# D times xc added by DVE, the gate multiplied by POOL: a diagonal matmul taken out of a state-space kernel

## Chip, cores and metric

The kernel runs on one core of one Trainium2 chip. The metric is the device time of one execution in microseconds. The engines are called as in the profile: PE is TensorE (its matmuls; PEld its weight loads), DVE is VectorE, ACT is ScalarE, POOL is GpSimd, SP is SyncE, which issues the DMAs.

## What is computed

16 samples of 64 x 64 positions and 96 channels pass two layers with residuals. Layer 0 normalizes by groups, resamples, and applies a quadratic between two matrices. Layer 1 is a selective state-space layer over the L = 4096 positions of a sample, with 192 inner channels and 16 states:

```python
xs, z = split(u @ W_in.T)
xc = silu(conv3(xs) + conv_b)
dt, Bm, Cm = split(xc @ W_x.T)
delta = softplus(dt @ W_dt.T + b_dt)
h = exp(delta * A) * h + delta * Bm * xc        # for each position in turn
y = sum_n(h * Cm) + xc * D
y = y * silu(z)
out = x + y @ W_out.T
```

The change concerns the last three lines: `+ xc * D`, the product with `silu(z)`, and when the product with `W_out` comes.

## The kernel before

**Tiling.** A sample is 8 chunks of T = 512 positions, so there are 128 chunks in all. A chunk has NU = 24 units: 192 channels x 16 states are 24 tiles of 128 rows by 512 positions. Three units form a group, 12 units a half (96 channels, `hf` 0 and 1).

**One unit.** ACT makes `av` (the exponential, L883). At the first unit of a group PE spreads B over 128 rows into the one PSUM bank `pb` (`spread_b`, L746), and DVE multiplies it with `rep_u` into `b3` for all three units (L1022, called b in the trace). For each unit DVE runs the scan into `hs` (L1028), POOL multiplies it by C into `hc` (L1069), and after each group PE sums over the states into the PSUM bank `py` (`reduce`, L757). At the start of each half PE first puts `diag(D)` times `xcs` into `py` (L754). When a half's four groups are summed, DVE multiplies `py` by `zs` = silu(z) into `xcs` (`gate`, L1036): half 0 after the scan of unit 15, half 1 after the scan of unit 3 of the next chunk.

**Order of work.** Every engine has one queue, and each is written out by one walk over chunks and units (`run`): the unit's own work, `c_part` (the chunk before), `a_part` (the chunk two ahead), and then the steps of a plan whose row is due. A row is a chunk's number times 24 plus a unit. `LAG` puts the steps later on the other engines than on PE (ACT by 6 units, DVE 3, POOL 2, SP 1). PE takes `spread_b` at units 1, 4, 7 and so on for the group that comes next, `reduce` at units 5 (group 0), 8, 11 and so on; groups 6 and 7 fall to units 23 and 2. `spread_b` must wait until DVE has read `pb` (`dve_bu`), and `b3` must wait for `pb`.

**Steps of the plan.** They share a ring of three PSUM banks `cb`; step i waits until step i - 3's bank is free. The steps are the resampling and the two matrices of layer 0 for samples ahead (S, W and D steps; W_f is L671, W_2 is L676, W_up is L665), the next chunks' X (L710), Z (L716), DBC (L720) and DT (L725) matmuls, with X and Z together at rows 8 and 9 of each chunk (the batch), and OUT, the output projection of the chunk before (L737 and L738), at row 6. OUT waits for both gates of its chunk (`dve_y`). ACT copies its bank to `os_` (L802), and SP stores it at its unit 13. The last sample has no S, W or D steps beside it, the one before it no S steps and W steps only until row 86.

The line numbers and functions:

Of the kernel before, what the change touches and what calls it, by code (L numbers as in the profile page):

```python
# [9 lines left out]
ALU = mybir.AluOpType  # L10
ACT = mybir.ActivationFunctionType

NS, HH, WW, C = 16, 64, 64, 96
# [9 lines left out]
NC8 = L // T  # L23
NJ, NQ = DI // 32, DSTATE // 4
NU = NJ * NQ
# [3 lines left out]
LEAD = 2  # L29
# [5 lines left out]
AT = {  # L35
    "pe": dict(pb=1, red=5),
    "act": dict(xn=8, mid=23, batch=BATCH + 6),
    "dve": dict(y0=15, y1=3),
    "pool": dict(u=23, bc=(16, 21)),
    "sp": dict(rd=(1, 2, 3, 5), ru=(6, 8, 10, 12), cs=(15, 16, 17, 18), dl=20, du=4, x1=21, out=13),  # L40
}
# [65 lines left out]
def plan_of(kind):  # L107
    rows = stage_rows(kind in ("first", "full"), kind in ("first", "full"), kind in ("first", "full", "tail"),
                      kind in ("first", "full", "tail"))
    for k in range(NC8):  # L110
        if kind != "last" or k < NC8 - LEAD:
            rows += mamba_rows(k)
        elif k == NC8 - LEAD:
            rows += mamba_rows(k, True)
        rows.append((k * NU + 6, ("PAD", -1) if kind == "first" and k == 0 else ("OUT", k)))
    if kind == "last":
        rows.append((NC8 * NU + 6, ("OUT", NC8)))
    return padded(rows)
# [22 lines left out]
def build(nc, A):  # L141
    ctx = ExitStack()
    with ctx:  # L143
        def sb(name, shape, dt=F32):
            return ctx.enter_context(nc.sbuf_tensor(name, shape, dt))
# [4 lines left out]
        def sem(name):  # L150
            return ctx.enter_context(nc.semaphore(name))
# [33 lines left out]
        dskip = sb("dskip", [C, 2])  # L185
        ddiag = sb("ddiag", [C, 2, C])
        selb = sb("selb", [C, NQ, 128], BF16)
# [102 lines left out]
        pe_red = sem("pe_red")  # L290
        dve_y = sem("dve_y")
        out_st = sem("out_st")

# [31 lines left out]
        SETUP_STEPS = 3  # L325
        N_SETUP = 14
        BEFORE = [alone([("SLD", 0)] + s_steps() + [("SG1", 0), ("SG2", 0)]),
# [76 lines left out]
        def count(sm, v):  # L404

            return max(v, 0)
# [194 lines left out]
        def _(pe):  # L601
# [125 lines left out]
            def out(st, k, bank):  # L727

                G = st.s * NC8 + k
                p = (k - 1) % 4  # L730
                pe.wait_ge(dve_y, count(dve_y, G * 2))
                pe.wait_ge(x1o_ld, count(x1o_ld, G * 16))
                for b in range(4):
                    tb = slice(128 * b, 128 * b + 128)
                    o = bank[:, C * b:C * b + C]
                    for t in range(2):
                        pe.matmul(o, xcs[:, p, t, tb], wo[:, t, :], start=(t == 0), stop=False)  # L737
                    mm = pe.matmul(o, x1o[:, tb], ident[0:C, 0:C], start=False, stop=True)  # L738
                return mm
# [8 lines left out]
            def reduce(s, k, g):  # L748
                G = s * NC8 + k
                hf, q = g // NQ, g % NQ  # L750
                pe.wait_ge(pool_hc, count(pool_hc, G * NU + 3 * g + 3))
                if q == 0:
                    pe.wait_ge(dve_y, count(dve_y, G * 2 + hf))
                    pe.matmul(py[0:C, :], ddiag[:, hf, :], xcs[:, k % 4, hf, :], start=True, stop=False,  # L754
                              skip_group_check=True)
                for j in range(3):
                    mm = pe.matmul(py[32 * j:32 * j + 32, :], rsel[:, :], hc[:, (3 * g + j) % NHC, :],  # L757
                                   start=False, stop=(q == NQ - 1), skip_group_check=True)
                mm.then_inc(pe_red, 1)
# [22 lines left out]
        def _(act):  # L782
# [63 lines left out]
            def batched(st, key, i):  # L846
# [11 lines left out]
                elif name == "Z":  # L858
                    t = key[2]
                    act.wait_ge(dve_y, count(dve_y, (G2 - LEAD) * 2))  # L860
                    act.wait_ge(pe_conv, st.done(i))
# [55 lines left out]
        def _(dve):  # L917
# [8 lines left out]
            def setup(ins):  # L926
                n_set[0] += 1
                ins.then_inc(setup_v, 1)
                dve.wait_ge(setup_v, count(setup_v, n_set[0]))
# [8 lines left out]
            for tap in range(3):  # L938
                setup(dve.tensor_tensor(wtap[:, tap, :, :], winx.rearrange("c (t p) -> c t p", t=2),
                                        cwb.rearrange("c (p t k) -> c k t p", t=2, k=3)[:, tap], ALU.mult))  # L940
            for t in range(2):
                setup(dve.tensor_scalar(ddiag[:, t, :], ident[0:C, 0:C], dskip[:, t:t + 1], None, ALU.mult))
            dve.wait_ge(setup_a, count(setup_a, 2))
# [69 lines left out]
            def unit(s, k, n):  # L1013
# [16 lines left out]
                if n == AT["dve"]["y0"]:  # L1030
                    gate(G, k, 0)

            def gate(G, k, hf):

                dve.wait_ge(pe_red, count(pe_red, G * NG + (hf + 1) * NQ))
                dve.tensor_tensor(xcs[:, k % 4, hf, :], zs[:, k % 2, hf, :], py[0:C, :], ALU.mult).then_inc(dve_y, 1)  # L1036

            def c_part(st, k, n):
                G = st.s * NC8 + k
                if n == AT["dve"]["y1"] and not (G < 1):  # L1040
                    gate(G - 1, (k - 1) % NC8, 1)

# [3 lines left out]
        def _(pool):  # L1046
# [56 lines left out]

            run(lambda row: row[0] + LAG["pool"], unit, step, a_part, lambda st, k, n: None)

# [67 lines left out]
```

## Time and profile before

| | |
|---|---|
| median of 3 runs | 7185.96 us (7182.05 to 7199.08) |
| the profiled execution | 7219.16 us, span 7217.5 us |
| busy, share of the span | PE 89%, DVE 82%, ACT 66%, POOL 63% |
| mean granted TensorE clock | 0.912 |
| first `b3` of the first chunk | 331.8 us |

The time is that of a whole execution; the span runs from the first to the last instruction in the profile. A busy share is the sum of an engine's instructions without overlaps. [...] The idle time in front of a group of instructions, with the engine that ended it, tells who waited for whom.

### The profile page before, as it was taken

The numbers are of one execution on the slowest core, as the hardware profiler recorded it, in microseconds if no ns is written. First come the engines' busy times: TensorE is split into PE (matmuls) and PEld (weight loads), VectorE is DVE, ScalarE is ACT, GpSimd is POOL, SyncE is SP. The second block draws the span as 40 slices with busy tenths as digits, with TensorE's granted clock in tenths as the row PEclk, the third lists the DMA queues.
The fourth block names the chain that finished last, engine by engine and source line by source line (L and its number), as shares of the span: only waits on it lengthen the run. The fifth ranks groups of instructions, "written<-read, shape, count | busy, mean of one in ns | idle before, by whom it ended". The sixth has DMA issues, their size and how long they took to land. (4 is left out here: it accounts for less than half of the span.)

```text
span 7217.5 us, 97516 instructions
## 1 busy us (share of the span) xinstructions
PE 6447.3 (89%) x32099; PEld 3299.1 (46%) x32099; DVE 5943.6 (82%) x4956; ACT 4794.1 (66%) x7986; POOL 4577.4 (63%) x4516
## 2 busy tenths in 40 slices
PE   7898998999898998999999899998999989898765
PEld 5545444444444444444444444444444444444211
DVE  0188888888888888888888888888888888889898
ACT  4576767667676776766667666676766767667554
POOL 0166666666666766667666666666766666677676
PEclk8998989999898998999999898998989999899776
DMA  3465655655655555565655555666555655555552
GB/s 89 112 151 134 146 141 129 148 136 146 148 136 141 140 143 137 145 147 131 150 130 147 143 134 140 138 150 144 136 146 132 150 137 145 144 129 142 121 122 68
DMA packets 805815, 983.15 MB, mean 136 GB/s; under 512 B 391258, under 2 KB 417542, under 8 KB 805318
## 3 DMA queue, kind: packets, MB, share of 16 engines
q1 hardware_dynamic: 805318, 976.92, 56.4%
q8 instruction: 264, 4.33, 0.3%
q14 instruction: 233, 1.91, 0.1%
HBM read 717.71 MB, written 259.00 MB: 135 GB/s over the span
## 5 line engine op out<-in xcount | busy, mean ns | idle before, releaser
L1069 POOL TENSOR_TENSOR hc<-hs,cs 128x512 f32<-128x512 f32 x3072 | 3843.5, 1269 | 2272.8 <-DVE hs L1028 1880.1
L1028 DVE TENSOR_TENSOR_SCAN hs<-av,state,b 128x512 f32<-128x512 f32 x2688 | 3282.4, 1264 | 83.5 <-DVE b L1022 2.7
L1022 DVE TENSOR_TENSOR b<-rep_u,pb 128x1536 f32<-128x1536 f32 x1024 | 1802.8, 1761 | 785.3 <-PE pb L746 721.2
L883 ACT ACTIVATE av<-rep_d,nega 128x512 f32<-128x512 f32 x3072 | 2129.2, 713 | 139.4 <-DVE hs L1028 134.9
L757 PE MATMUL py<-hc,rsel 128*32 128x512 f32 x6144 | 1227.4, 678 | 27.3 <-POOL hc L1069 27.2
L676 PEld LDWEIGHTS cb<-w2c,g 128*98 128x98 f32 x9600 | 937.6, 178 | 330.2 <-issue 267.9
L671 PE MATMUL cb<-xu,w1a 96*128 96x392 f32 x2400 | 1039.9, 529 | 50.1 <-ACT dlt L873 31.0
L676 PE MATMUL cb<-w2c,g 128*98 128x96 f32 x9600 | 990.2, 264 | 83.2 <-issue 55.4
L833 ACT ACTIVATE g<-cb,b1a 128x392 f32<-128x392 f32 x1200 | 695.7, 580 | 205.3 <-PE cb L671 189.5
L746 PE MATMUL pb<-bc,selb 96*128 96x512 bf16 x1024 | 416.4, 407 | 370.0 <-DVE b L1022 368.6
L710 PE MATMUL cb<-xn,wtap 96*96 96x512 f32 x1536 | 701.0, 606 | 0.3 <-DVE spare L966 0.3
L671 PEld LDWEIGHTS cb<-xu,w1a 96*128 96x128 f32 x2400 | 409.4, 194 | 547.8 <-issue 350.6
L1028 DVE TENSOR_TENSOR_SCAN hs<-av,zero_state,b 128x512 f32<-128x512 f32 x384 | 468.1, 1264 | 12.2 <-ACT av L883 0.6
L710 PEld LDWEIGHTS cb<-xn,wtap 96*96 96x96 f32 x1536 | 243.5, 165 | 468.7 <-issue 467.3
L857 ACT ACTIVATE xcs<-cb,tapb 96x512 f32<-96x512 f32 x256 | 174.9, 683 | 409.9 <-PE cb L710 409.9
L757 PEld LDWEIGHTS py<-hc,rsel 128*32 128x32 f32 x6144 | 161.8, 113 | 620.0 <-issue 449.4
L665 PE MATMUL cb<-up_h,t1r 128*96 128x196 f32 x1600 | 362.6, 351 | 50.7 <-DVE b1a L1000 46.8
L826 ACT ACTIVATE vr<-cb 98x384 f32<-98x384 f32 x400 | 194.3, 486 | 305.4 <-PE cb L676 304.0
L746 PEld LDWEIGHTS pb<-bc,selb 96*128 96x128 bf16 x1024 | 107.1, 105 | 618.2 <-DVE b L1022 393.3
L754 PE MATMUL py<-xcs,ddiag 96*96 96x512 f32 x512 | 296.3, 663 | 95.2 <-DVE xcs L1036 71.9
L737 PE MATMUL cb<-wo,xcs 96*128 96x96 f32 x2048 | 346.5, 297 | 0.8 <-issue 0.8
L826 ACT ACTIVATE xu<-cb 96x392 f32<-96x392 f32 x400 | 194.1, 485 | 221.5 <-PE cb L665 219.5
(102 smaller groups left out, 6525.5 us busy)
## 6 DMA issues: line engine op xcount, KB each, us to landing
rep_d<-delta_scratch SPq DMA_DIRECT2D x512, 384.0 KB, 6.2
rep_u<-deltax_scratch SPq DMA_DIRECT2D x512, 384.0 KB, 6.1
cs<-c_scratch SPq DMA_DIRECT2D x512, 256.0 KB, 6.1
delta_scratch<-dlt SPq DMA_DIRECT2D x128, 384.0 KB, 3.1
deltax_scratch<-dlt SPq DMA_DIRECT2D x128, 384.0 KB, 8.1
t_scratch<-t1s SPq DMA_DIRECT2D x128, 300.0 KB
t1r<-t_scratch SPq DMA_DIRECT2D x160, 240.0 KB, 5.0
rr<-v_scratch SPq DMA_DIRECT2D x256, 150.0 KB
```

Of the source, the lines that this page charges most:

```text
L665: mm = pe.matmul(bank[0:C, e * 2 * GH:(e + 1) * 2 * GH], t1r[:, m % 2, i2 % 5, :], up_h[:, :], start=True, stop=True)
L671: mm = pe.matmul(bank[:, 0:BC], w1a[:, 128 * f:128 * f + 128], xu[:, b % 2, :], start=True, stop=True)
L676: mm = pe.matmul(bank[0:GH, C * j:C * j + C], g2[:, b % 2, f, GH * j:GH * j + GH], w2c[:, f, :], start=(f == 0), stop=(f == NF - 1))
L710: mm = pe.matmul(bank[0:C, :], wtap[:, tap, t, :], xn[:, k2 % 2, tap:tap + T], start=(tap == 0), stop=(tap == 2))
L746: pe.matmul(pb[:, :], selb[:, g % NQ, :], bc3[:, k % 4, :], start=True, stop=True).then_inc(pe_b, 1)
L757: mm = pe.matmul(py[32 * j:32 * j + 32, :], rsel[:, :], hc[:, (3 * g + j) % NHC, :], start=False, stop=(q == NQ - 1), skip_group_check=True)
L826: act.activation(out, src, ACT.Copy).then_inc(fr, 1)
L833: act.activation(g2[:, b % 2, f, :], bank[:, 0:BC], ACT.Square, bias=b1a[:, f:f + 1]).then_inc(fr, 1)
L883: act.activation(av[:, n % NAV, :], rep_d[:, k % 2, j, :], ACT.Exp, scale=nega[:, q, j:j + 1])\
L1022: dve.tensor_tensor(b3[:, :, :], rep_u[:, k % 2, 3 * hf:3 * hf + 3, :], pb[:, None, :].broadcast_to([128, 3, T]), ALU.mult).then_inc(dve_b ...
L1028: dve.tensor_tensor_scan(hs[:, n % NHS, :], av[:, n % NAV, :], b3[:, n % 3, :], start, ALU.mult, ALU.add)\
L1069: pool.tensor_tensor(hc[:, n % NHC, :], hs[:, n % NHS, :], cs[:, k % 2, g % NQ, :], ALU.mult)\
```

## The change

`ddiag` and its two setup operations go, and with them the matmul L754; the first `reduce` of a half now starts the accumulation. DVE's `gate` becomes `skip`: it reads `py`, adds `D * xcs` in the same instruction and writes `xcs`. POOL multiplies both halves of `xcs` by `zs` in one instruction of 96 x 1024, at its unit 4 of the next chunk, behind that unit's product. OUT and ACT's Z wait for POOL's new semaphore `pool_y` in place of `dve_y`. OUT goes from row 6 to row 7 and SP's store from unit 13 to 14; PE's queue at row 7 has `spread_b` of group 3 first and then the steps, so OUT is now behind it.

```diff
-    "pool": dict(u=23, bc=(16, 21)),
-    "sp": dict(rd=(1, 2, 3, 5), ru=(6, 8, 10, 12), cs=(15, 16, 17, 18), dl=20, du=4, x1=21, out=13),
+    "pool": dict(u=23, bc=(16, 21), gate=4),
+    "sp": dict(rd=(1, 2, 3, 5), ru=(6, 8, 10, 12), cs=(15, 16, 17, 18), dl=20, du=4, x1=21, out=14),
...
-        rows.append((k * NU + 6, ("PAD", -1) if kind == "first" and k == 0 else ("OUT", k)))
+        rows.append((k * NU + 7, ("PAD", -1) if kind == "first" and k == 0 else ("OUT", k)))
...
-                pe.wait_ge(dve_y, count(dve_y, G * 2))
+                pe.wait_ge(pool_y, count(pool_y, G))
                 pe.wait_ge(x1o_ld, count(x1o_ld, G * 16))
...
                 if q == 0:
                     pe.wait_ge(dve_y, count(dve_y, G * 2 + hf))
-                    pe.matmul(py[0:C, :], ddiag[:, hf, :], xcs[:, k % 4, hf, :], start=True, stop=False,
-                              skip_group_check=True)
                 for j in range(3):
                     mm = pe.matmul(py[32 * j:32 * j + 32, :], rsel[:, :], hc[:, (3 * g + j) % NHC, :],
-                                   start=False, stop=(q == NQ - 1), skip_group_check=True)
+                                   start=(q == 0), stop=(q == NQ - 1), skip_group_check=True)
...
                     t = key[2]
-                    act.wait_ge(dve_y, count(dve_y, (G2 - LEAD) * 2))
+                    act.wait_ge(pool_y, count(pool_y, G2 - LEAD))
...
-            def gate(G, k, hf):
+            def skip(G, k, hf):
 
                 dve.wait_ge(pe_red, count(pe_red, G * NG + (hf + 1) * NQ))
-                dve.tensor_tensor(xcs[:, k % 4, hf, :], zs[:, k % 2, hf, :], py[0:C, :], ALU.mult).then_inc(dve_y, 1)
+                dve.scalar_tensor_tensor(out=xcs[:, k % 4, hf, :], in0=xcs[:, k % 4, hf, :], scalar=dskip[:, hf:hf + 1],
+                                         in1=py[0:C, :], op0=ALU.mult, op1=ALU.add).then_inc(dve_y, 1)
...
+            def c_part(st, k, n):
+                G = st.s * NC8 + k
+                if n == AT["pool"]["gate"] and G >= 1:
+
+                    pool.wait_ge(dve_y, count(dve_y, G * 2))
+                    pool.tensor_tensor(xcs[:, (k - 1) % 4], xcs[:, (k - 1) % 4], zs[:, (k - 1) % 2], ALU.mult).then_inc(pool_y, 1)
```

## Rows read from the trace of the kernel before

**Rows 1.** The page, part 1: busy us of the whole execution, share, instructions.

```profile
PE 6447.3 (89%) x32099; PEld 3299.1 (46%) x32099; DVE 5943.6 (82%) x4956; ACT 4794.1 (66%) x7986; POOL 4577.4 (63%) x4516
```

**Rows 2.** The waits: who waited for whom, us in total, times, longest.

```profile
DVE b L1022 <- PE pb L746: 721.2, 321, 8.2
...
PE pb L746 <- DVE b L1022: 368.6, 169, 5.4
```

**Rows 3.** Groups of instructions by shape: busy and mean ns, idle before, releasers.

```profile
L1028 DVE TENSOR_TENSOR_SCAN hs<-av,state,b 128x512 f32<-128x512 f32 x2688 | 3282.4, 1264 | 83.5 <-DVE b L1022 2.7 <-POOL state L1073 0.4
...
L1102 POOL TENSOR_TENSOR dlt<-dlt,xcs 96x1024 f32<-96x1024 f32 x128 | 301.5, 2355 | 26.4 <-DMA delta_scratch<-dlt 24.3 <-PE py L757 2.1
L754 PE MATMUL py<-xcs,ddiag 96*96 96x512 f32 x512 | 296.3, 663 | 95.2 <-DVE xcs L1036 71.9 <-POOL hc L1069 21.7
...
L1036 DVE TENSOR_TENSOR xcs<-zs,py 96x512 f32<-96x512 f32 x256 | 169.4, 662 | 31.0 <-PE py L757 31.0
...
L984 DVE SCALAR_TENSOR_TENSOR vv<-dm,mv 96x1 f32<-96x1 f32 x32 | 34.4, 1074 | 1.1
```

**Rows 4.** Windows: full samples, then from 6680 us: busy by engine, clock, DMA, GB/s.

```profile
763.50:6680.00 5916.50, 5417.95 (x27270) 2793.33 (x27273) 5064.20 (x4191) 4059.74 (x6790) 3909.88 (x3852) 0.93 0.59 141
6680.00:7217.50 537.50, 353.18 (x1198) 111.53 (x1192) 480.73 (x377) 276.93 (x405) 375.36 (x374) 0.72 0.44 102
```

**Rows 5.** Timeline of the last sample, chunk at 6919 us: start us, us, engine, instruction.

```profile
6928.91 1.99 PE L754 MATMUL py<-xcs,ddiag 96*96 96x512 f32 x2 [1.42 <-DVE xcs L1036]
...
6930.04 2.49 POOL L1069 TENSOR_TENSOR hc<-hs,cs 128x512 f32<-128x512 f32 x2 [0.36 <-DVE hs L1028]
...
6930.83 1.93 PE L757 MATMUL py<-hc,rsel 128*32 128x512 f32 x6
6931.23 1.76 DVE L1022 TENSOR_TENSOR b<-rep_u,pb 128x1536 f32<-128x1536 f32 x1
...
6932.69 0.89 PE L737 MATMUL cb<-wo,xcs 96*128 96x96 f32 x4
...
6935.65 0.38 PE L746 MATMUL pb<-bc,selb 96*128 96x512 bf16 x1
...
6936.95 5.39 PE L710 MATMUL cb<-xn,wtap 96*96 96x512 f32 x12
...
6944.31 1.76 DVE L1022 TENSOR_TENSOR b<-rep_u,pb 128x1536 f32<-128x1536 f32 x1 [2.02 <-PE pb L746]
```

**Rows 6.** Windows in the same chunk, before and after the clock rises.

```profile
6919.60:6933.10 13.50, 7.33 (x18) 1.40 (x19) 13.02 (x11) 4.80 (x8) 12.62 (x13) 0.50 0.82 185
6933.20:6944.30 11.10, 11.10 (x51) 5.34 (x52) 8.90 (x7) 5.10 (x8) 7.71 (x8) 1.00 0.87 183
```

**Rows 7.** PE in a chunk with the output projection at 1.2 GHz: timeline, window.

```profile
5791.05 1.06 PE L737 MATMUL cb<-wo,xcs 96*128 96x96 f32 x4
...
5796.17 0.63 PE L746 MATMUL pb<-bc,selb 96*128 96x512 bf16 x1
...
5789.90:5796.30 6.40, 6.40 (x34) 6.26 (x32) 0.00 (x0) 0.47 (x1) 0.21 (x2) 0.50 0.57 151
```

**Rows 8.** Timeline of a sample's last chunk, from 5504 us.

```profile
5514.41 1.10 PE L754 MATMUL py<-xcs,ddiag 96*96 96x512 f32 x2 [1.30 <-POOL hc L1069]
5514.45 3.72 POOL L1069 TENSOR_TENSOR hc<-hs,cs 128x512 f32<-128x512 f32 x3
...
5515.92 1.76 DVE L1022 TENSOR_TENSOR b<-rep_u,pb 128x1536 f32<-128x1536 f32 x1
...
5517.19 0.58 PE L737 MATMUL cb<-wo,xcs 96*128 96x96 f32 x4
```

**Rows 9.** Timeline around units 17 to 24 of the chunk at 5606 us.

```profile
5646.78 1.02 PE L754 MATMUL py<-xcs,ddiag 96*96 96x512 f32 x2
...
5651.77 1.76 DVE L1022 TENSOR_TENSOR b<-rep_u,pb 128x1536 f32<-128x1536 f32 x1 [1.18 <-PE pb L746]
...
5659.89 1.76 DVE L1022 TENSOR_TENSOR b<-rep_u,pb 128x1536 f32<-128x1536 f32 x1 [1.19 <-PE pb L746]
```

More of the change, by code:

```diff
@@ L114, in plan_of @@
             rows += mamba_rows(k, True)
-        rows.append((k * NU + 6, ("PAD", -1) if kind == "first" and k == 0 else ("OUT", k)))
+        rows.append((k * NU + 7, ("PAD", -1) if kind == "first" and k == 0 else ("OUT", k)))
     if kind == "last":
-        rows.append((NC8 * NU + 6, ("OUT", NC8)))
+        rows.append((NC8 * NU + 7, ("OUT", NC8)))
     return padded(rows)
@@ L185, in build @@
         dskip = sb("dskip", [C, 2])
-        ddiag = sb("ddiag", [C, 2, C])
         selb = sb("selb", [C, NQ, 128], BF16)
@@ L291, in build @@
         dve_y = sem("dve_y")
+        pool_y = sem("pool_y")
         out_st = sem("out_st")
@@ L325, in build @@
         SETUP_STEPS = 3
-        N_SETUP = 14
+        N_SETUP = 12
         BEFORE = [alone([("SLD", 0)] + s_steps() + [("SG1", 0), ("SG2", 0)]),
@@ L940, in _ @@
                                         cwb.rearrange("c (p t k) -> c k t p", t=2, k=3)[:, tap], ALU.mult))
-            for t in range(2):
-                setup(dve.tensor_scalar(ddiag[:, t, :], ident[0:C, 0:C], dskip[:, t:t + 1], None, ALU.mult))
             dve.wait_ge(setup_a, count(setup_a, 2))
@@ L1030, in unit @@
                 if n == AT["dve"]["y0"]:
-                    gate(G, k, 0)
-            def gate(G, k, hf):
+                    skip(G, k, 0)
+            def skip(G, k, hf):
                 dve.wait_ge(pe_red, count(pe_red, G * NG + (hf + 1) * NQ))
-                dve.tensor_tensor(xcs[:, k % 4, hf, :], zs[:, k % 2, hf, :], py[0:C, :], ALU.mult).then_inc(dve_y, 1)
+                dve.scalar_tensor_tensor(out=xcs[:, k % 4, hf, :], in0=xcs[:, k % 4, hf, :], scalar=dskip[:, hf:hf + 1],
+                                         in1=py[0:C, :], op0=ALU.mult, op1=ALU.add).then_inc(dve_y, 1)
             def c_part(st, k, n):
@@ L1040, in c_part @@
                 if n == AT["dve"]["y1"] and not (G < 1):
-                    gate(G - 1, (k - 1) % NC8, 1)
+                    skip(G - 1, (k - 1) % NC8, 1)
             run(lambda row: row[0] + LAG["dve"], unit, step, lambda st, k, n: None, c_part)
@@ L1102, in a_part @@
                     pool.tensor_tensor(dlt[:, :, :], dlt[:, :, :], xcs[:, k2 % 4], ALU.mult).then_inc(pool_u, 1)
-            run(lambda row: row[0] + LAG["pool"], unit, step, a_part, lambda st, k, n: None)
+            def c_part(st, k, n):
[3 more added lines that the diff above has]
+                    pool.tensor_tensor(xcs[:, (k - 1) % 4], xcs[:, (k - 1) % 4], zs[:, (k - 1) % 2], ALU.mult).then_inc(pool_y, 1)
+            run(lambda row: row[0] + LAG["pool"], unit, step, a_part, c_part)
 def resampling():
```

## Prediction

> **What bounds the kernel now.** I read four views in this order. The page's first part says that no engine is full: PE 89%, DVE 82%, POOL 63% [rows 1]. So the bound must change hands inside each chunk, and the waits say between whom: DVE waits 721 us for `pb` from PE (321 times), and PE waits 369 us for DVE to release the single `pb` buffer (169 times) [rows 2]. Who is late where, the timelines tell. A chunk (24 units, 8 groups, 128 chunks) has two halves. In groups 0 to 2 DVE leads and PE waits for it. Then PE has the output projection, reduction 1 and the batch of X and Z matmuls in a row, and group 4's `b` is late in every chunk: in the chunk at 6919 us DVE idles 2.02 us before it [rows 5]. So what PE does between the first gate of a chunk and group 4 is on the path; most of what it does in groups 0 to 2 is not. The last view is TensorE's clock: 0.93 on average while a sample has all its side work, 0.72 from 6680 us on [rows 4]. In the chunk at 6919 us it is 0.50 (1.2 GHz) up to 6933.1 us, where DVE waits for nobody, and 1.00 (2.4 GHz) right after, in the stretch that is on the path [rows 6]. Where the clock rises thus matters as much as how much work there is.
>
> **The change, part by part.**
>
> *The diagonal matmuls go.* 256 of them (512 records). The two records took 1.02 us at 2.4 GHz [rows 9] and 1.99 us at 1.2 GHz [rows 5]; the group's sum is 296 us [rows 3]. As PE's work overlaps by some 0.07 us from group to group, each is worth 0.95 us of PE's time at 2.4 GHz. The second one of a chunk (unit 17) lies where PE comes late to groups 7 and 0: the chunk at 5606 us shows DVE idle 1.18 us before group 7's `b` and 1.19 us before the next group 0's [rows 9]. The same two places in the eight chunks from 5553 to 5987 us: in four chunks such a wait is over 1 us in at least one of them, in two about 0.6 us, in two nothing; so 4 x 0.95 + 2 x 0.5 = 4.8 us a sample, and with 14 samples that have side work -67 us. Ends: 0, if the time goes into other waits, and 8 x 0.95 x 14 = -106 us. I take -67.
>
> *The first diagonal matmul and the moved output, at an unchanged clock.* The projection goes from row 6 (before `pb` of group 3) to row 7 (behind it). So PE no longer fills the time until `b` of group 2 has released `pb`. At 5504 us and later: `b` ends at 5515.92 + 1.76 = 5517.68. PE began the projection at 5517.19; without the diagonal it is there 1.0 us earlier, at 5516.2, and now stands until 5517.7, 1.5 us [rows 8]. Then come `pb` and a W step, and the projection waits for POOL: unit 4's product ends at 5514.45 + 2.5 = 5516.95, the new multiply has the shape of L1102, 2.36 us [rows 3], so 5519.3 us. It starts 2.1 us later than before and has `pb` and that W step (0.8 us together, an estimate) behind it already, so group 4 comes 1.3 us later. In the other seven chunks the waits come to 0 to 1.3 us and are paid with the diagonal's 0.95 us: from a gain of 0.9 (fourth chunk, where PE comes late anyway) to a loss of 0.2. Sum over a sample about +0.3 us with this chunk, x 14 = +4 us; ends -14 and +28 us.
>
> *The clock.* This is the term on which I decide. In the chunk at 6919 us PE works from 6928.91 us without a pause: diagonal 1.99 us, reduction 0 1.93 us, and the clock rises at about 6933.1 us, as the projection has begun; projection, reduction 1 and batch then run at 2.4 GHz [rows 5, 6]. After the change PE has reduction 0 alone, then stands 2.2 us until `b` of group 2 ends at 6932.99 us, does `pb`, and starts the projection at 6930.04 + 1.26 + 2.36 = 6933.7 us, 1.0 us later than before. Does the projection itself raise the clock? Rows say no: from 5789.9 to 5796.3 us PE was busy without a gap, nearly all of it projection, and the clock stayed 0.50; the projection took 5796.17 - 5791.05 = 5.1 us in place of 6935.65 - 6932.69 = 3.0 us [rows 5, 7]. So I expect +1.0 (later start), +2.1 (projection at 1.2 GHz), +0.9 (reduction 1, 1.93 us in place of 1.06) and about +1 for the part of the batch before the rise (between 0 and the batch's whole 5.4 us): 5.0 us for each of some 9 chunks without W and S work at the end. +45 us; ends +9 (clock as before) and +90.
> [...]
> In the 14 full samples the same can happen wherever PE now pauses before the projection. Most exposed is each sample's last chunk, [rows 8]: pauses of 1.30 us before reduction 0, then 1.5 us and a short third one, with little work between. Next are the seventh and the second with 0.9 to 1.6 us. If the clock falls there, the loss is that of above without its first term, 4 to 5 us. I take 1.3 such losses a sample at 4.5 us: 6 us x 14 = +84 us; ends 0 and 3 a sample, +189 us.
>
> *DVE's new operation.* `skip` reads one tile of SBUF and one of PSUM, as the gate did (662 ns) and as the scan does [rows 3]; it has two arithmetic steps and a pointer scalar more. A scan has a pointer scalar too and takes its 1264 ns next to a busy POOL. I take 0 to 60 ns for each of 256, half of them where DVE is on the path: +8 us; ends 0 and +15.
> The nearest operation of the same name, L984, takes 1074 ns for one element [rows 3]. [...]
>
> *POOL.* 128 multiplies of 2.36 us more, 302 us; POOL goes from 63% to 67%. They stand before unit 5's product and put it off by 2.4 us. Reduction 1 needs it, but now follows the projection, 2.8 us or more later; group 3's scans need its buffers some 2 us after it is ready. Cost nothing; without that cover it would be up to 2.4 us a chunk. ACT's Z (unit 14) waits for POOL's product of unit 4, done long before. The queues that OUT is moved past: ACT has one exponential more before it, SP stores `os_` one unit later; both ran ahead. At the very end the multiply stands alone on the path: +2 us.
>
> **Sum.** -67 + 4 + 45 + 84 + 8 + 2 = +76 us. The profiled execution took 7219.2 us (span 7217.5), so its like would take about 7295; the median of the three runs is 33 us lower, and I add the difference to it: 7186 + 76 = 7262 us.
>
> **Rivals.**
> *Less work for PE, faster.* All as above but for the clock, which keeps its level in full samples: -67 + 4 + 9 to 24 + 8 + 2 = -44 to -29 us, and with the second diagonal paying in every chunk -85: 7100 to 7157, say 7140 us. For it: PE is the busiest engine and DVE waits for it twice as long as the other way [rows 1, 2]. Against: the pauses of [rows 8]. It decides when a sample has fewer than about 0.6 such losses (0.6 x 4.5 x 14 = 38 us).
> *They cancel.* Between half a loss and one a sample, or DVE as the bound everywhere: 7165 to 7207 us, say 7186.
> [...]
> *The change does not do what it says:* the diagonal goes, but the rows saved are waited away at `pb`. That is the case "cancel" without clock, included there.
>
> **Chances.** Slower by the clock 0.55, the port 0.02, cancel 0.16, faster 0.27. 0.3% (22 us) is about what a measurement here can tell from no change. Likeliest 7262, its own range 7210 to 7350. Faster cases reach down to 7100; I leave 1 in 10 out below 7120 and 1 in 10 above 7350.
>
> **What the next profile would show.** Right: no L754; in the chunks after 6680 us the clock is still 0.50 while the projection runs, it takes about 5 us there, and the idle time before group 4's `b` grows from 2.0 to about 7 us; the idle time before group 3's vanishes; DVE's total wait for `pb` rises from 721 us towards 800, PE's wait for DVE too; the mean clock falls below 0.91. POOL's multiply 2.36 us, `skip` 660 to 720 ns. The wait before groups 7 and 0 shrinks by about 1 us where it was larger. Wrong, if the clock rises before the projection after all, or if the last chunk of a sample keeps 2.4 GHz: then 7140. [...]

## The result, and the profile after

| | median | runs |
|---|---|---|
| before | 7186.33 us | 5 |
| after | 7463.32 us | 5 (7429.8 to 7471.32) |

The ratio is 1.0366, 95% interval 1.0347 to 1.0386: 277 us slower. The direction is as forecast, the size is 3.6 times the forecast's 76 us. The profiled execution of after took 7429.8 us (span 7428.0), 210.6 us more than the one of before; it is the quickest of its five, so the traces hold 211 of the 277 us. The mean granted clock, TensorE's share of its full speed, fell from 0.912 to 0.873. Where the prediction and the expectations write 1.2 and 2.4 GHz, the windows show a granted clock of 0.50 and of 1.00 [rows 6]; no view gives a frequency. One of before's later executions took 7324 us at a clock of 0.868; it is set apart as slow and stands in no ratio below.

The page of after, part 1, and the waits that answer to [rows 2]:

```profile
PE 6458.6 (87%) x31587; PEld 3386.2 (46%) x31587; DVE 5957.0 (80%) x4954; ACT 4798.8 (65%) x7986; POOL 4866.4 (66%) x4644
```

```profile
DVE b L1018 <- PE pb L746: 903.6, 271, 15.6
...
PE pb L746 <- DVE b L1018: 481.4, 277, 5.4
```

PE has 512 matmuls fewer and is busy 11 us longer: the diagonal's 296 us [rows 3] are gone, and the remaining matmuls take 308 us more. They are the same instructions at a mean granted clock of 0.873 in place of 0.912: L737, for one, is busy 413.5 us where it was 346.5. DVE waits 182 us more for `pb` in fewer waits (271, before 321); the longest is 15.6 us where it was 8.2. Added up by the group of the `b` that waits, the idle time of DVE before group 4's grew from 415 to 719 us, the one before group 3's fell from 134 to 44, and the one before groups 7 and 0 together from 141 to 102. So the loss lies where the projection and the batch are. The groups of after, by shape:

```profile
L737 PE MATMUL cb<-wo,xcs 96*128 96x96 f32 x2048 | 413.5, 339 | 12.2 <-issue 11.7
...
L1106 POOL TENSOR_TENSOR xcs<-xcs,zs 96x1024 f32<-96x1024 f32 x128 | 301.3, 2354 | 2.7 <-DVE xcs L1032 2.7
...
L694 PE MATMUL cb<-xt,wtot 96*96 96x256 f32 x512 | 194.5, 468 | 55.8 <-DMA rr<-v_scratch 51.2 <-DMA xt<-xt_scratch 2.8
L1032 DVE SCALAR_TENSOR_TENSOR xcs<-xcs,dskip,py 96x512 f32<-96x512 f32 x256 | 184.9, 722 | 31.8 <-PE py L755 31.8
```

and L694 in before:

```profile
L694 PE MATMUL cb<-xt,wtot 96*96 96x256 f32 x512 | 187.8, 454 | 15.9 <-DMA rr<-v_scratch 10.7 <-DMA xt<-xt_scratch 3.3
```

The multiply takes the 2.36 us of the forecast, `skip` 722 ns (60 more than the gate, the upper end). The surprise is L694, the first matmul of a D step: over the whole run it waits 51.2 us for its DMA `rr`, before 10.7 us. The windows answer to [rows 4]; the clock is the number after POOL's busy time:

```profile
763.50:6860.00 6096.50, 5437.72 (x26925) 2873.35 (x26924) 5093.19 (x4206) 4071.66 (x6802) 4169.09 (x3974) 0.89 0.58 137
6860.00:7428.00 568.00, 356.80 (x1098) 120.28 (x1096) 470.32 (x367) 273.97 (x398) 393.53 (x378) 0.62 0.40 93
```

The clock of 0.93 has become 0.89 in the full samples, and 0.72 has become 0.62 at the end.

**Where the time went.** The traces were cut into chunks, from the start of group 0's `b` to the next. Places in a sample are counted from 1 (first chunk, sixth chunk), samples and chunks of the run from 0. "Projection" is the time from OUT's first matmul to its last: in after's trace 2.8 to 2.9 us in the 67 chunks where the granted clock was 1.00 over all of it, 5.3 to 5.4 in the 44 where it was 0.50 (16 had both). Means over the 13 samples 1 to 13, by place in the sample, us:

| chunk of the sample | 1 | 2 | 3 | 4 | 5 | 6 | 7 | 8 | sum |
|---|---|---|---|---|---|---|---|---|---|
| before, chunk | 54.2 | 53.7 | 51.6 | 56.3 | 63.7 | 54.5 | 50.0 | 51.0 | 435.1 |
| after, chunk | 52.2 | 52.5 | 51.1 | 56.1 | 64.8 | 62.5 | 52.9 | 54.2 | 446.3 |
| before, OUT starts at | 14.1 | 14.0 | 14.1 | 16.0 | 23.6 | 15.1 | 15.6 | 13.9 | |
| after, OUT starts at | 16.0 | 14.9 | 14.5 | 17.7 | 24.5 | 21.2 | 16.7 | 15.1 | |
| before, projection | 2.8 | 2.8 | 2.8 | 2.8 | 5.1 | 2.8 | 2.8 | 3.4 | |
| after, projection | 2.8 | 2.8 | 2.8 | 2.8 | 5.3 | 5.3 | 3.8 | 4.9 | |

13 x 11.2 = 146 us. The last sample but one takes 427.8 us in place of 404.2, the first seven chunks of the last 365.5 in place of 332.5: 57 us. Together 202 of 211 us; 8 lie in sample 0 and at the ends. The largest entry is the sixth chunk, 8.0 us in each of these samples. This is one of them (it starts at 5950.18 us) on PE in after's timeline:

```profile
5965.00 0.39 PE L746 MATMUL pb<-bc,selb 96*128 96x512 bf16 x1 [0.44 <-DVE b L1018]
5965.23 0.82 PE L671 MATMUL cb<-xu,w1a 96*128 96x392 f32 x2
5969.37 1.14 PE L694 MATMUL cb<-xt,wtot 96*96 96x256 f32 x2 [3.32 <-DMA rr<-v_scratch]
5970.31 1.49 PE L698 MATMUL cb<-dn_w,rr 100*96 100x96 f32 x8
5971.59 1.06 PE L737 MATMUL cb<-wo,xcs 96*128 96x96 f32 x4
...
5976.85 1.93 PE L755 MATMUL py<-hc,rsel 128*32 128x512 f32 x6
5978.70 7.32 PE L710 MATMUL cb<-xn,wtap 96*96 96x512 f32 x12
5985.86 1.88 PE L716 MATMUL cb<-xn,winz 96*96 96x512 f32 x4
```

and on DVE:

```profile
5987.99 1.76 DVE L1018 TENSOR_TENSOR b<-rep_u,pb 128x1536 f32<-128x1536 f32 x1 [13.38 <-PE pb L746]
```

The same chunk in before's timeline (it starts at 5831.52 us), PE and then DVE:

```profile
5846.60 0.58 PE L737 MATMUL cb<-wo,xcs 96*128 96x96 f32 x4
...
5849.25 0.38 PE L746 MATMUL pb<-bc,selb 96*128 96x512 bf16 x1
5849.47 0.82 PE L671 MATMUL cb<-xu,w1a 96*128 96x392 f32 x2
5851.69 0.64 PE L694 MATMUL cb<-xt,wtot 96*96 96x256 f32 x2 [1.40 <-DMA rr<-v_scratch]
...
5853.93 5.39 PE L710 MATMUL cb<-xn,wtap 96*96 96x512 f32 x12
```

```profile
5861.29 1.76 DVE L1022 TENSOR_TENSOR b<-rep_u,pb 128x1536 f32<-128x1536 f32 x1 [5.40 <-PE pb L746]
```

The reader is to see the order. Row 7 holds `pb`, then a W step (L671), then a D step (L694, L698) that waits for `rr`. Before, the projection stood ahead of all of it and filled most of the time until `rr` came; the D step waited 1.40 us. After, the projection is queued behind the wait, now 3.32 us, starts 6 us later, and comes out of the pause at a granted clock of 0.50. Windows of after, over the pause with what PE did just ahead of it, over the projection, and (last two) in the end-of-run chunk shown next:

```profile
5965.10:5968.90 3.80, 0.95 (x3) 0.32 (x2) 3.80 (x4) 1.57 (x3) 3.69 (x4) 1.00 0.95 199
5970.50:5977.20 6.70, 6.70 (x36) 6.37 (x37) 4.02 (x4) 0.66 (x2) 0.00 (x0) 0.50 0.74 169
...
7114.60:7132.70 18.10, 15.74 (x44) 7.82 (x45) 13.08 (x10) 4.43 (x7) 13.38 (x13) 0.50 0.71 160
7132.90:7137.00 4.10, 4.10 (x11) 1.34 (x9) 0.00 (x0) 1.31 (x3) 0.00 (x0) 1.00 0.13 27
```

That chunk (start 7105.20 us) answers to [rows 5]; timeline of after:

```profile
7114.70 1.93 PE L755 MATMUL py<-hc,rsel 128*32 128x512 f32 x6 [1.49 <-DVE xcs L1032]
...
7117.04 2.35 POOL L1106 TENSOR_TENSOR xcs<-xcs,zs 96x1024 f32<-96x1024 f32 x1
...
7118.83 0.61 PE L746 MATMUL pb<-bc,selb 96*128 96x512 bf16 x1 [2.21 <-DVE b L1018]
...
7119.50 1.14 PE L737 MATMUL cb<-wo,xcs 96*128 96x96 f32 x4
...
7124.83 1.93 PE L755 MATMUL py<-hc,rsel 128*32 128x512 f32 x6
...
7126.69 8.46 PE L710 MATMUL cb<-xn,wtap 96*96 96x512 f32 x12
...
7137.12 1.76 DVE L1018 TENSOR_TENSOR b<-rep_u,pb 128x1536 f32<-128x1536 f32 x1 [9.05 <-PE pb L746]
```

PE stands 1.49 and 2.21 us, the projection starts as POOL's multiply ends, and the granted clock stays at 0.50 until 7132.8 us, through the projection, reduction 1 and the first 6.1 of L710's 8.46 us. Group 4's `b` waits 9.05 us for `pb` where it waited 2.02 [rows 5].

### The profile page after: what moved, and what is told of

Same layout as the page of the kernel before. It is cut to its first block and busy times, and to the rows that moved or that the text cites. A ratio compares the mean times of both kernels' runs of the same rounds, so it can differ in the third digit from the quotient of the medians.

```text
span 7428.0 us, 96643 instructions
## 1 busy us (share of the span) xinstructions
PE 6458.6 (87%) x31587; PEld 3386.2 (46%) x31587; DVE 5957.0 (80%) x4954; ACT 4798.8 (65%) x7986; POOL 4866.4 (66%) x4644
## 3 DMA queue, kind: packets, MB, share of 16 engines
q1 hardware_dynamic: 805318, 976.92, 55.2%
## 5 line engine op out<-in xcount | busy, mean ns | idle before, releaser
L755 PE MATMUL py<-hc,rsel 128*32 128x512 f32 x6144 | 1278.4, 704 | 120.0 <-DVE xcs L1032 72.3
L676 PEld LDWEIGHTS cb<-w2c,g 128*98 128x98 f32 x9600 | 960.7, 182 | 359.3 <-issue 241.1
L676 PE MATMUL cb<-w2c,g 128*98 128x96 f32 x9600 | 1014.7, 267 | 110.9 <-issue 54.9
L671 PE MATMUL cb<-xu,w1a 96*128 96x392 f32 x2400 | 1041.0, 530 | 49.2 <-ACT dlt L871 31.0
L710 PE MATMUL cb<-xn,wtap 96*96 96x512 f32 x1536 | 746.5, 638 | 0.0
L671 PEld LDWEIGHTS cb<-xu,w1a 96*128 96x128 f32 x2400 | 411.2, 195 | 548.2 <-issue 352.9
L710 PEld LDWEIGHTS cb<-xn,wtap 96*96 96x96 f32 x1536 | 259.2, 177 | 532.3 <-issue 532.0
L737 PE MATMUL cb<-wo,xcs 96*128 96x96 f32 x2048 | 413.5, 339 | 12.2 <-issue 11.7
L737 PEld LDWEIGHTS cb<-wo,xcs 96*128 96x128 f32 x2048 | 373.5, 253 | 46.0 <-issue 38.7
L800 ACT ACTIVATE os_<-cb 128x384 f32<-128x384 f32 x128 | 62.8, 490 | 482.8 <-PE cb L738 482.8
```

Of the source, the lines that this page charges most:

```text
L671: mm = pe.matmul(bank[:, 0:BC], w1a[:, 128 * f:128 * f + 128], xu[:, b % 2, :], start=True, stop=True)
L676: mm = pe.matmul(bank[0:GH, C * j:C * j + C], g2[:, b % 2, f, GH * j:GH * j + GH], w2c[:, f, :], start=(f == 0), stop=(f == NF - 1))
L710: mm = pe.matmul(bank[0:C, :], wtap[:, tap, t, :], xn[:, k2 % 2, tap:tap + T], start=(tap == 0), stop=(tap == 2))
```

## The experiments

Three theories were set against each other. *Clock:* the loss is TensorE running at a granted clock of 0.50 behind pauses that the change puts ahead of the projection. *Queue:* the projection stands behind something that waits. *POOL:* the projection or the Z copies wait for the new multiply. Row 6.5 stands for a place in row 7 behind `pb` of group 3 but ahead of that row's S, W and D steps. Each kernel was timed beside before, whose median in these rounds was 7192 to 7205 us, not 7186; the ratios and their intervals are the measure, and a difference of less than 20 us between two rows of the table says little. "Under 4 us" counts the projections, of the 104 in samples 1 to 13, that were.

| kernel | diagonal | OUT | multiply | median us | ratio, 95% | under 4 us |
|---|---|---|---|---|---|---|
| before | yes | row 6 | DVE | 7186 | | 89 |
| E13 | yes | 6.5 | DVE | 7243.56 | 1.0050 (1.0025, 1.0075) | 95 |
| E2 | yes | row 7 | DVE | 7322.39 | 1.0190 (1.0159, 1.0221) | 80 |
| E6 | no | row 6 | DVE | 7095.57 | 0.9861 (0.9828, 0.9895) | 97 |
| E8 | no | row 7 | DVE | 7428.34 | 1.0318 (1.0286, 1.0350) | 66 |
| E4 | yes | row 7 | POOL | 7397.37 | 1.0289 (1.0250, 1.0327) | 76 |
| E10 | yes | row 6 | POOL | 7401.82 | 1.0274 (1.0251, 1.0296) | 83 |
| after | no | row 7 | POOL | 7463 | 1.0366 (1.0347, 1.0386) | 59 |
| E1 | no | row 6 | POOL | 7432.00 | 1.0341 (1.0318, 1.0364) | 69 |
| E5 | no | 6.5 | POOL | 7393.32 | 1.0264 (1.0237, 1.0291) | 73 |
| E3 | no | row 6 | POOL, unit 3 | 7169.36 | 0.9951 (0.9931, 0.9970) | 88 |
| E9 | no | row 6 | POOL, by halves | 7110.63 | 0.9874 (0.9846, 0.9902) | 90 |
| E11 | no | row 6 | POOL, idle matmuls | 7296.07 | 1.0123 (1.0085, 1.0162) | 94 |
| E12 | no | row 6 | as E9, some idle matmuls | 7096.16 | 0.9847 (0.9819, 0.9874) | 95 |

**E1: after, the projection back in row 6.**

```diff
-    "pool": ..., "sp": dict(..., out=14),
+    "pool": ..., "sp": dict(..., out=13),
-        rows.append((k * NU + 7, ... ("OUT", k)))
+        rows.append((k * NU + 6, ... ("OUT", k)))
```

> The changed kernel with the output projection back in row 6 (and SP's store at unit 13); DVE's skip, POOL's multiply and the missing diagonal stay. Theory A, the place: with the changed kernel the projection lies behind that row's D step, which waits 3.3 us for a DMA in the sixth chunk of each sample, PE stands, and the clock is at 1.2 GHz when the projection starts (21.2 to 26.4 us of the chunk, b of group 4 at 36.6 in place of 28.9 us). With row 6 the sixth chunk gets about 8 us back and the fifth 1 us, 14 times: 7463 - 126 = about 7340 us, between 7300 and 7380. Not all comes back, since the projection still waits for POOL. Theory B, POOL: the projection waits for POOL's multiply wherever it stands, and in row 6 it holds up the spread of group 3 too: no gain, 7460 us or more. Theory C, less work for PE by itself lets the clock fall: no gain from the place, 7440 to 7480 us.

Measured: 7432.0, only 31 us under after and in none of the three ranges that were expected (7300 to 7380, 7460 or more, 7440 to 7480). The sixth chunk is back at 55.2 us, so the queue in it is gone; but the second takes 56.5 (before 53.7), the seventh 53.9, the eighth 56.3, with projections of 4.2, 4.1 and 5.3 us. What the projection now waits for is POOL, and PE stands meanwhile: the idle time before L737 without a named releaser is 162 us on PE's matmuls and 234 on their weight loads, in the kernel without the multiply (E6, below) 1 and 24. One place of E1's trace in the last sample ties it to POOL, whose multiply ends at 7111.64 + 2.34 = 7113.98 us:

```profile
7111.64 2.34 POOL L1106 TENSOR_TENSOR xcs<-xcs,zs 96x1024 f32<-96x1024 f32 x1
```

```profile
7114.08 1.14 PE L737 MATMUL cb<-wo,xcs 96*128 96x96 f32 x4 [2.87 <-issue]
```

**E2: before, the projection in row 7** (the reverse of E1's edit, on the old kernel).

> The kernel before with one edit: the output projection in row 7 (and SP's store at unit 14); diagonal matmuls and DVE's gate stay. Theory A, the place: the sixth chunk of each sample loses about 8 us as in the changed kernel, 14 x 8 = 112 us: about 7300 us, between 7260 and 7340; at the end of the run, where there is no side work, nothing, as diagonal and reduction 0 still raise the clock before the projection. Theory B, POOL, and theory C, less work for PE: neither is in this kernel, so 7186 us within 22 us.

Measured: +136 us with nothing else changed. Its sixth chunk takes 62.4 us (projection starts at 20.7, takes 5.3); the end-of-run chunks stay at 47.8 us, with the granted clock at 1.00 over their projections. In this execution the place alone costs the sixth chunk and little else; E13 shows an execution in which the end of the run pays too.

**E4: after, with the diagonal matmuls back on PE** (`skip` stays, with a scalar of zero; `ddiag` and its setup, not shown, come back too).

```diff
+                    pe.matmul(py[0:C, :], ddiag[:, hf, :], xcs[:, k % 4, hf, :], start=True, stop=False, ...)
-                                   start=(q == 0), stop=(q == NQ - 1), skip_group_check=True)
+                                   start=False, stop=(q == NQ - 1), skip_group_check=True)
-                dve.scalar_tensor_tensor(..., scalar=dskip[:, hf:hf + 1],
+                dve.scalar_tensor_tensor(..., scalar=zero2[:, hf:hf + 1],
```

> The changed kernel with the two diagonal matmuls of a chunk back on PE; DVE's skip stays the same instruction but its scalar is zero, so the output is the reference's and only PE's work differs. Clock theory (C, and part of A): in the chunks at the end of the run diagonal and reduction 0 keep PE at work together and the clock is up sooner; these chunks lose about 1 us in place of 5, some 9 x 4 = 36 us less, and the last chunks of samples some more; against it the second diagonal costs up to 2 us a chunk x 4 a sample again. Faster than the changed kernel, 7380 to 7440 us, with the chunks at the end near 49 us in place of 52 to 55. Rival, PE's work is what counts: each diagonal costs its 0.95 us where PE is late, 7463 + 60 to 120 us = 7520 to 7580 us.

Measured: 7397.4. More work for PE, 66 us less time than after. The gain is where projections are quick again (seventh chunk 51.3 us with a projection of 2.8, after 52.9 with 3.8; eighth 51.8 with 3.4, after 54.2 with 4.9); the chunks of the last sample did not change (51.9 to 54.9 us up to the sixth, in after 51.9 to 55.3), where 49 was expected.

**E6: before, without the diagonal matmuls.** The reduction's first matmul starts the accumulation instead. This kernel, and E8 after it, leaves the term `D * xc` out of the output; they price a removal and are no candidates.

```diff
-                    pe.matmul(py[0:C, :], ddiag[:, hf, :], xcs[:, k % 4, hf, :], start=True, stop=False, ...)
-                                   start=False, stop=(q == NQ - 1), skip_group_check=True)
+                                   start=(q == 0), stop=(q == NQ - 1), skip_group_check=True)
```

> The kernel before without the diagonal matmuls; nothing takes their place, so the term D times xc is left out of the output. It shows what the removal alone is worth. Forecast of the prediction's terms: second diagonal -67 us, first one near 0, and at the end of the run the clock is low when the projection starts, about +2 us x 9 chunks: 7140 us, between 7100 and 7180. Rival, the clock: with less work PE's clock falls in full samples as well, and the removal is worth nothing or a loss: 7190 to 7280 us.

Measured: 7095.6, 91 to 103 us under before, 4 us below the expected range. In a full sample 11.5 us are gained (423.6); the last sample loses 18 (first seven chunks 350.3 us, before 332.5): its projections start 1.9 us earlier and take 5.44 in place of 3.1: in before the granted clock was 0.93 over the projection, with the diagonal ahead of it, and here it is 0.50 (from 6932.69 us in before and from 6785.51 us in E6).

**E3: E1 with POOL's multiply ahead of unit 3's product** (`gate=3`).

> The changed kernel with the projection in row 6 and POOL's multiply one unit earlier (behind unit 3's product in place of unit 4's), so that the projection can start some 1.3 us sooner: at about 12.5 us of a chunk in place of 14.2 to 15.0. Theory, the wait: what costs in row 6 is not POOL's work but that PE stands before the projection until POOL has multiplied (projection at 14.3 to 15.1 us in place of 12.4 to 13.3 us without the multiply) and the clock falls there. Then most of the 336 us between the kernel without multiply and diagonal in row 6 (7096) and the one with the multiply (7432) comes back: 7160 to 7230 us, the chunks at the end of the run near 51 us. Rival, POOL's work: 2.36 us more a chunk on POOL delays its products and with them PE and DVE, wherever the multiply stands: 7380 us or more.

Measured: 7169.4, 263 us under E1 for a multiply of the same length: in the end-of-run chunks the projection starts at 12.60 us in place of 14.29, 1.7 us earlier.

**E5: after, the projection at row 6.5**: behind `pb` of group 3, but ahead of row 7's W and D steps.

> The changed kernel with the projection still behind the spread of group 3 in row 7, but ahead of that row's S, W and D steps, not behind them. Theory, the D step: only in the sixth chunk does the place in row 7 cost much, since a D step that waits 3.3 us for a DMA lies ahead of the projection there; now the projection fills that wait. The sixth chunk goes from 62.5 us to about 56, 14 x 6.5 = 91 us: 7370 us, between 7330 and 7410. Rival, the pause before the spread of group 3: it is still there, so 7440 to 7480 us, sixth chunk 60 us or more.

Measured: 7393.3. The sixth chunk is 55.0 us. So its loss comes from the steps of row 7 ahead of the projection, and `pb` is not the cause. That it is the D step among them, the wait for `rr` says: 51.2, 43.5, 47.2 and 51.9 us in the four kernels with the output in row 7 (after, E2, E4, E8), 9 to 24 us in the kernels with it in row 6 or 6.5.

**E8: E6 with the projection in row 7.**

> The kernel before without the diagonal matmuls (the term D times xc is left out of the output) and with the projection in row 7; DVE's gate as before, no multiply on POOL. If removal (-103 us) and place (+136 us) simply add up: 7186 + 33 = 7219 us, between 7195 and 7245. If without the diagonal PE's pause before the spread of group 3 makes the clock fall, more: 7260 to 7340 us, with the seventh and eighth chunks over 51 us. What is then missing to the changed kernel (7463) belongs to POOL's multiply.

Measured: 7428.3, above the higher of the two ranges expected. The removal that gained some 100 us in row 6 loses 106 in row 7. Its projections take 5.3 us in the end-of-run chunks (54.6 us each, E6 49 to 52), in 7 of 13 seventh chunks and in 9 of 13 eighth ones. Some 43 of the 106 us are the last sample (434.9 us, E2 392.0), and that part can come and go by itself, as E13 shows.

**E9: E1 with POOL's multiply taken apart**, half 0 at unit 18 of its own chunk, half 1 at unit 3 of the next.

```diff
-    "pool": dict(u=23, bc=(16, 21), gate=4),
+    "pool": dict(u=23, bc=(16, 21), gate=3, gate0=18),
...
-                pe.wait_ge(pool_y, count(pool_y, G))
+                pe.wait_ge(pool_y, count(pool_y, G * 2))
...
+            def mul(G, k, hf):
+                pool.wait_ge(dve_y, count(dve_y, G * 2 + hf + 1))
+                pool.tensor_tensor(xcs[:, k % 4, hf, :], xcs[:, k % 4, hf, :], zs[:, k % 2, hf, :], ALU.mult)\
+                    .then_inc(pool_y, 1)
```

> A repair: diagonal on DVE and multiply on POOL as in the changed kernel, projection in row 6, but POOL multiplies the halves apart: half 0 behind unit 18's product of its own chunk, half 1 behind unit 3's of the next, 96 x 512 each. Only some 1.2 us of POOL stand then between DVE's last skip and the projection, which can start at about 11.4 us of a chunk. Theory, the wait: the projection waits almost nowhere and the time is that of the kernel without the diagonal (7096) plus up to 40 us: 7096 to 7140 us, faster than before. Rival, POOL's work: 7300 us or more.

Measured: 7110.6, 321 us under E1 with the same work on PE and DVE. The halves take 1267 ns each, the projection starts at 11.5 us at the end of the run, and DVE's wait for `pb` is 618 us:

```profile
DVE b L1018 <- PE pb L746: 618.3, 253, 8.2
```

**E10: E4 with the projection in row 6.**

> The cell of the table that is missing: diagonal matmuls on PE (DVE's skip with a zero scalar, so the output is the reference's), projection in row 6, multiply on POOL behind unit 4. Theory, pause and clock: without the diagonal this place costs 336 us with POOL's multiply, because PE stands 1 to 3 us before the projection; the diagonal fills 1 us of the pause in every chunk (2 us at 1.2 GHz) and keeps the clock. So little more than the direct wait is left, 0.2 to 0.5 us in most chunks and 1 us at the end of the run: 7230 us, between 7200 and 7290, faster than the same kernel without the diagonal (7432) although PE has 256 matmuls more. Rival, POOL's wait as such costs the 336 us: 7500 us or more.

Measured: 7401.8. The expectation was missed by 170 us: the diagonal does not protect a projection that waits for POOL. Its projections start at 14.29 us at the end of the run, as in after, E1, E4 and E5, and take 5.41, at a granted clock of 0.50. They start 1.1 us later than in before, and the first six chunks of the last sample are 4.5 to 5.7 us longer than its 47.8; so of this loss 1.1 us a chunk is the direct wait and by estimate 3.4 to 4.6 the clock.

**E11: E1 with two idle matmuls in front of the projection's wait for POOL.** They write to the bank that the step is to fill; the output is unchanged.

```diff
+                for _ in range(2):
+                    pe.matmul(bank[0:C, 0:HID], ident[0:C, 0:C], w1t[:, :], start=True, stop=True)
                 pe.wait_ge(pool_y, count(pool_y, G))
```

> The kernel of the first experiment (row 6, no diagonal, multiply on POOL behind unit 4: 7432 us) with two more matmuls in each projection step, before it waits for POOL: 96 x 384 float32, into the step's own bank, which the projection then overwrites; nothing reads them. Pure added work, 1.5 us at 2.4 GHz and 2.9 us at 1.2 GHz a chunk. Clock theory: they keep PE at work in the pause, the projection and the batch run at 2.4 GHz more often, and the kernel gets faster by adding work: 7250 to 7350 us, the chunks at the end of the run at 49 to 50 us in place of 53. Rival, without the clock: where PE stood less than 1.5 us the work is simply added, 0.5 to 1 us a chunk: 7480 to 7560 us.

Measured: 7296.1, 136 us faster than E1 by more work: 214 us of idle matmuls, and PE busy 6436.5 us in place of 6453.7. In the means over samples 1 to 13 the projections start up to 0.7 us later than in E1, in the fifth chunk 1.9 us. Two chunks of its last sample show the clock apart from everything else. PE's timeline in the chunk that starts at 6877.81 us:

```profile
6887.31 1.93 PE L757 MATMUL py<-hc,rsel 128*32 128x512 f32 x6 [1.49 <-DVE xcs L1034]
6889.16 2.26 PE L732 MATMUL cb<-w1t,ident 96*96 96x384 f32 x4
6892.06 0.69 PE L739 MATMUL cb<-wo,xcs 96*128 96x96 f32 x4 [0.63 <-POOL xcs L1108]
...
6894.81 0.38 PE L748 MATMUL pb<-bc,selb 96*128 96x512 bf16 x1
6895.12 1.06 PE L757 MATMUL py<-hc,rsel 128*32 128x512 f32 x6
6896.11 5.39 PE L710 MATMUL cb<-xn,wtap 96*96 96x512 f32 x12
...
6903.06 0.38 PE L748 MATMUL pb<-bc,selb 96*128 96x512 bf16 x1
```

and in the next, from 6926.48 us:

```profile
6935.98 1.93 PE L757 MATMUL py<-hc,rsel 128*32 128x512 f32 x6 [1.48 <-DVE xcs L1034]
6937.83 2.88 PE L732 MATMUL cb<-w1t,ident 96*96 96x384 f32 x4
6940.73 1.17 PE L739 MATMUL cb<-wo,xcs 96*128 96x96 f32 x4
...
6946.52 1.93 PE L757 MATMUL py<-hc,rsel 128*32 128x512 f32 x6
6948.38 5.53 PE L710 MATMUL cb<-xn,wtap 96*96 96x512 f32 x12
...
6955.47 0.38 PE L748 MATMUL pb<-bc,selb 96*128 96x512 bf16 x1
```

The windows of the two:

```profile
6892.20:6903.20 11.00, 11.00 (x48) 5.40 (x48) 8.29 (x7) 4.95 (x7) 8.83 (x10) 1.00 0.81 175
6938.00:6950.50 12.50, 12.48 (x40) 7.25 (x41) 9.36 (x8) 2.99 (x4) 8.42 (x9) 0.57 0.63 135
```

The same program, the same pauses, the projection at 14.25 us after the chunk's start in both. In the first the clock rises during the idle matmuls (2.26 us at a mean granted clock of 0.66, in place of 2.88 at 0.50) and group 4's `pb` starts 6903.06 - 6877.81 = 25.3 us into the chunk; in the second it does not, and `pb` starts at 29.0. The chunks take 48.7 and 52.4 us. So the clock alone is worth 3.7 us of a chunk here.

**E12: E9 with the two idle matmuls in the last 11 projections only.**

```diff
+                for _ in range(2 if G >= 8 * NS - 11 else 0):
```

> The repair with halves (7111 us) and the two idle matmuls of the kernel beside it, but only in the last eleven projection steps, where PE has no side work and the chunks take 50.2 to 52.7 us in place of the 47.8 us of the kernel before. Clock theory: these chunks come to 48.5 us, 11 x 2.3 = 25 us: 7085 us, between 7070 and 7110. Rival, without the clock: 11 x 1 to 2 us more, 7120 to 7135 us.

Measured: 7096.2; the first seven chunks of the last sample take 333.8 us, in E9 353.5, and the sample before it 402.9, in E9 393.6. The intervals of the two ratios overlap, so the idle matmuls' own gain is not settled. Either is 1.3 to 1.5% faster than before.

**E13: before, the projection at row 6.5.**

> The kernel before (diagonal on PE, gate on DVE) with the projection in row 7 behind the spread of group 3, but ahead of that row's S, W and D steps. Theory, the D step: of the 136 us that row 7 costs the kernel before (7322), nearly all is the sixth chunk, where a D step that waits for a DMA stands ahead of the projection; with the diagonal PE pauses before the spread for 0.3 us only. So 7186 to 7215 us, sixth chunk 54 to 56 us in place of 62.4. Rival, the pause before the spread of group 3 costs by itself: 7280 us or more, over all chunks.

Measured: 7243.6 (10 runs, 7189 to 7263), ratio 1.005: 79 us under E2, but 29 us above the range that was expected. The sixth chunk is 54.5 us as in before, so what E2 lost there is the D step ahead of the projection. Samples 1 to 13 take 432.7 us each, 2.4 less than in before. The profiled execution, the slowest of the ten, loses at the end: the first seven chunks of the last sample take 375.8 us in place of 332.5, six of them 54.6 in place of 47.8, with projections of 5.3 us.

This last sample is the clearest sight of the clock in all runs. It has no S, W or D steps, so rows 6.5 and 7 mean the same there, and PE's instructions in its first seven chunks are the same 736 records, in the same order, in E2's trace and in E13's. E2 took 332.9 us for them with projections of 2.8 us at a granted clock of 1.00 (from 6938.91 us), E13 375.8 with projections of 5.3 at 0.50 (from 6840.08 us). So one and the same queue order ran the end of the run with its projections at either clock, for 43 us. The runs of the two kernels fall apart in the same way: E13's are 7189, 7193 and 7203, then 7241 to 7263; E2's are 7319 to 7325, then 7361. Only one of each was profiled, so that the others split for this reason is not shown.

## Why the forecast was right in direction and wrong in size

*The step that failed* is the one that priced the moved output outside the clock: "In the other seven chunks the waits come to 0 to 1.3 us". It reckoned the projection as moved past `pb`, and past a W step in the last chunk of a sample. In the sixth chunk row 7 also has a D step, and its wait for `rr` had been covered by the projection. The chunk goes from 54.5 to 62.5 us, 8.0 us in each of 13 samples and 6.6 in sample 0: 111 us, where the term had +4 for everything. E2 pays it on the old kernel, E5 and E13 avoid it, which puts it on the row's steps, and the waits for `rr` put it on the D step. The views would have shown it: before's own D step waited 1.40 us there with 2.8 us of projection ahead of it. About 2.5 of the 8.0 us are the projection at a granted clock of 0.50 behind that pause (5.3 in place of 2.8 us), some 6 the later start, less what has moved ahead of it. Without this chunk the traces would hold a loss of 100 us, so the direction does not hang on it.

*The clock in full samples* was +84 us by 1.3 losses a sample. The seventh and eighth chunks lost 2.9 and 3.2 us, 6.1 a sample or 85 us, with 7 and 12 of 13 projections slow in place of 0 and 3. The kind of loss and its size hold, though the forecast was a guess at a count and put most of it on the eighth chunk. That the clock has a part in it beside the wait is shown on E1's kernel: idle work in the same pause gives back 136 us (E11).

*The end of the run* was +45 us (5.0 us for each of nine chunks). Measured 57 over the last two samples. In E2 and E13, without POOL's multiply, the projections of the last sample ran at a granted clock of 1.00 and of 0.50. With the multiply at unit 4 and no idle matmuls all five profiled kernels (after, E1, E4, E5, E10) ran them at 0.50, in 5.41 us. The steps hold in kind: reduction 0 alone, a stand of 2.21 us (2.2 forecast), the projection at 14.3 us, 1.1 later than in before (1.0 forecast), 5.4 us long (5.1). The part of the batch at a clock of 0.50 was put at about 1 us; L710 took 8.46 in place of 5.39, so 3 us in this chunk. The idle time before `b` went from 2.0 to 9.05 us here (7 forecast); over the chunks 119 to 125 (of 128, counted from 0) the loss is 4.1 to 7.5 us each.

*The second diagonal*, -67 us. Of the eight chunks that the forecast counted, before's trace has a wait of over 1 us before group 7 or the next group 0 in three (from 5553, 5606 and 5937 us), not four, so its own sum gives (3 x 0.95 + 2 x 0.5) x 14 = -54. Chunks 1 to 4 gained 2.0, 1.3, 0.5 and 0.2 us, 56 us in 14 samples, both diagonals and the new pauses together. The fifth chunk, which no term named, lost 1.1 us (10 us in 14 samples). E6 shows what the removal alone is worth: 11.5 us in a full sample.

*POOL*, "cost nothing". Nearly true as long as the projection is in row 7: E8 to after is +35 us. But the multiply bounds where the projection can be. With it at unit 4 the projection starts at 14.29 us in the last sample (after, E1, E4, E5, E10; 14.25 in E11), with the output in row 6 and no multiply at 11.29 (E6). With the output in row 6 the same multiply costs 336 us (E6 to E1), of which E9 gets 321 back by its place.

*`skip`*: 722 ns (715 to 745 over all 256), the upper end of 0 to 60 more; 256 x 60 = 15 us of DVE's time, of which no run shows what is on the path. The 0.02 that the prediction gives to the port rests on a wait of `skip` for POOL, which no run shows: the `skip` at 725.59 us took 718 ns with POOL busy all the while.

*The rival "faster"* had its point of decision right. E6, which takes work from PE and moves nothing, is 1.4% faster, and E9, which computes the whole output, 1.3%. The +24 us at the upper end of its clock term, for the end of the run, is shown by no run; there after lost 57 us, and E6 18. What was put wrong is to sum the edits. In us, the diagonal's removal is worth

| | projection in row 6 | in row 7 |
|---|---|---|
| multiply on DVE | -91 to -103 | +106 |
| multiply on POOL | +30 | +66 |

(E6, E8, E1, after against before, E2, E10, E4, their partners with the diagonal). Without the diagonal, row 7 alone costs 333 us (E6 to E8), the multiply alone 336 (E6 to E1), and both 368 (E6 to after). Each opens a pause ahead of the same short block, and the second pause costs 32 to 35 us more.

*What stays open.* 66 of the 277 us are between the profiled and the median executions, and no trace holds them. What tips the end of the run to one clock or the other in E2 and E13 was not found either, nor whether before's own end, at the quick clock in the one profiled execution, is always so. In full samples, direct waiting for POOL and the clock were not taken apart.

## What to carry to other kernels

Before a block of work is moved in an engine's queue, list each instruction that it now stands behind in every chunk of the period, and look for one that waits with the block as its cover; here one place of eight cost 111 of the 211 us. In this kernel work taken from TensorE was worth its time (91 to 103 us) only where no other edit opened a pause ahead of what is on the path; behind such a pause its removal cost 106, 30 and 66 us (E8, E1, after), with a mean granted clock of 0.870, 0.872 and 0.873 where the same kernels with the work in place had 0.906, 0.895 and 0.894 (E2, E10, E4). So fill the pause (136 us here), or move the late producer (here a multiply split in halves, 321 us), before removing work. The edits did not add up here (333 and 336 us each alone, 368 together), so time such edits in pairs.

## What the runs showed of the hardware that was not expected

- The profile shows PE busy for 6.70 of 6.70 us from 5970.5 us in after, with the D step's L698 and the projection, and the granted clock was 0.50 throughout. [rows 7] shows the same over 6.40 of 6.40 us.
- With two idle matmuls ahead of the projection more of the projections were quick: 94 of 104 under 4 us in E11, 69 in E1.
- Two identical chunks side by side differed in the clock alone, 3.7 us of 49 (E11, granted clock 1.00 and 0.50 over the projection), and the same 736 matmuls in the same order took 332.9 us in one kernel's trace and 375.8 in another's (E2, E13).
- DVE's `scalar_tensor_tensor` with one input in SBUF and one in PSUM took 722 ns for 512 elements beside a POOL busy 66% of the span, 60 ns over before's plain product of the same size; the one with both inputs in SBUF took 1074 on average for a single element [rows 3].
